# Layer 1's rotation: the halves of the partitions exchanged by ScalarE, one sine product on VectorE

## The reference, cut to what matters

```python
def _rope(x):
    ...
    freqs = jnp.repeat(freqs, 2, axis=-1)
    cos, sin = (jnp.cos(freqs), jnp.sin(freqs))
    x2 = x.reshape(*x.shape[:-1], DQ // 2, 2)
    rot = jnp.stack([-x2[..., 1], x2[..., 0]], axis=-1).reshape(x.shape)
    return x * cos + rot * sin
...
q = _rope(q)
k = _rope(k)
...
scores = scores + _alibi(t)[None]
scores = scores / math.sqrt(DQ)
scores = 30.0 * jnp.tanh(scores / 30.0)
...
probs = jax.nn.softmax(scores, axis=-1)
```

## Time and profile before

| what | value |
|---|---|
| median of 3 runs | 904.81 us (902.95 to 905.9) |
| profiled execution | 901.0 us, span 899.2 us |
| mean granted TensorE clock | 0.949 |
| PE / DVE / ACT / POOL busy | 804.3 / 626.3 / 448.5 / 466.3 us |
| chain that ended last | PE 67%, DVE 16%, POOL 7%, ACT 5% |

### The profile page before, as it was taken

One profiled execution on the slowest core, in us unless ns is written; L12 is line 12 of the kernel. 1 busy time (PEld: TensorE's weight loads), 2 busy tenths in 40 slices (PEclk: granted clock), 3 DMA queues, 4 the chain that ended last, 5 costly groups with the idle time before them and its releaser, 6 DMA issues.

```text
span 899.2 us, 13733 instructions
## 1 busy us (share of the span) xinstructions
PE 804.3 (89%) x4707; PEld 637.1 (71%) x4707; DVE 626.3 (70%) x1115; ACT 448.5 (50%) x795; POOL 466.3 (52%) x506
## 2 busy tenths in 40 slices
PE   2999999988787858998999897989999999999996
PEld 2866666663232246687888797979989998888874
DVE  8387757368988866789868884767766755555556
ACT  3322232188766622667645554555646552555541
POOL 3556736244654525445635547685866432565550
PEclk9999999997868987999999998999999999999999
DMA  4111192000000012000000001110110377754307
GB/s 173 54 52 35 53 315 75 1 1 0 1 1 1 2 37 107 25 7 7 25 7 19 7 18 49 31 48 25 48 36 25 115 166 286 216 150 117 95 3 233
DMA packets 50115, 59.80 MB, mean 67 GB/s; under 512 B 13559, under 2 KB 41084, under 8 KB 50048
## 3 DMA queue, kind: packets, MB, share of 16 engines
q1 hardware_dynamic: 45488, 50.49, 18.6%
q0 software_dynamic: 4560, 8.44, 2.6%
HBM read 41.11 MB, written 21.86 MB: 70 GB/s over the span
## 4 chain that ended last, share of the span: by engine, by line
PE 67%; DVE 16%; POOL 7%; ACT 5%; issue 4%; DMA 1%; SPq 0%; DVEq 0%; ACTq 0%; POOLq 0%
PE ps L452 11%; PE ps L454 10%; PE ps L453 10%; PE ps L693 9%; PE ps L778 7%; PE ps L596 6%; PE ps L802 3%; DVE A L1245 3%; DVE cap L1319 2%; DVE swap L1309 2%; PE ps L533 2%; PE ps L516 2%; PE ps L759 2%; PE ps L491 1%; POOL cT_lo L1633 1%
## 5 line engine op out<-in xcount | busy, mean ns | idle before, releaser
L993 ACT ACTIVATE cap<-cap 128x1024 f32<-128x1024 f32 (+7 forms) x128 | 86.8, 678 | 139.8 <-DVE cap L1319 139.5
L693 PE MATMUL ps<-V,P 128*128 128x129 f32 x1152 | 154.4, 281 | 0.0
L693 PEld LDWEIGHTS ps<-V,P 128*128 128x128 f32 x1152 | 147.1, 196 | 3.0
L1319 DVE SCALAR_TENSOR_TENSOR cap<-dist,ps 128x1024 f32<-128x1024 f32 (+7 forms) x128 | 95.9, 750 | 37.8 <-PE ps L454 25.8
L1529 POOL TENSOR_SCALAR_AFFINE_SELECT P<-P 128x128 f32<-128x128 f32 x128 | 38.5, 303 | 129.3 <-ACT P L998 129.1
L1659 POOL DMA_INDIRECT y_scratch<-y_sb,aux_s x63 | 62.0, 984 | 55.8 <-issue 38.9
L998 ACT ACTIVATE P<-cap 128x1024 f32<-128x1024 f32 (+7 forms) x128 | 87.6, 685 | 4.1
L452 PE MATMUL ps<-q_hi,k_hi 128*128 128x512 f32 x192 | 73.4, 382 | 4.1 <-DVE cap L1319 3.9
L1245 DVE TENSOR_TENSOR A<-A 128x1024 f32<-128x1024 f32 (+4 forms) x60 | 63.0, 1102 | 8.8 <-ACT A L942 8.5
L778 PE MATMUL ps<-ew,xT 128*128 128x256 f32 (+1 forms) x252 | 66.7, 387 | 2.6 <-ACT xT L1023 1.3
L454 PE MATMUL ps<-q_lo,k_hi 128*128 128x512 f32 x192 | 68.8, 358 | 0.0
(11 more groups left out here) (266 smaller groups left out, 2075.8 us busy)
## 6 DMA issues: line engine op xcount, KB each, us to landing
xg_scratch<-blank SPq DMA_DIRECT2D x1, 8127.0 KB, 31.7
xa<-xg_scratch SPq DMA_DIRECT2D x63, 128.0 KB
ew<-in_experts SPq DMA_DIRECT2D x3, 1920.0 KB, 7.7
ew<-in_experts SPq DMA_DIRECT2D x2, 2688.0 KB, 10.1
y<-y_scratch SPq DMA_DIRECT2D x8, 512.0 KB, 5.2
pk<-in_packed SPq DMA_DIRECT2D x8, 384.0 KB, 3.0
pks<-in_scales SPq DMA_DIRECT2D x8, 384.0 KB, 3.8
wqk<-in_wqk SPq DMA_DIRECT2D x20, 128.0 KB
```

The source lines that it names most:

```text
L693: last = pe.matmul(ps[:, 4 + r % 2, o:o + D1 + 1], P1[:, h % 2, a:a + P], V1[:, j, h // REP, :], start=(j == 0), stop=(j == t))
L993: act.activation(cap[:, n % 2, 0:w], cap[:, n % 2, 0:w], ACT.Tanh, scale=1.0 / (CAP * float(D1) ** 0.5))\
L1319: dve.scalar_tensor_tensor(out=cap[:, n % 2, 0:w], in0=dist[:, 0:w], scalar=slope, in1=psf[:, 1024 * (n % 2):1024 * (n % 2) + w], op0=ALU. ...
```

## The change

ScalarE gets a step for every projection, `swap_halves`: it waits for the projection and copies the upper half of the bank's partitions to the lower half of `swap` and the lower to the upper. VectorE waits for these copies (`pj_turned`) in place of the projection itself, multiplies the bank by the cosines as before, and then multiplies `swap` in place by the sines, in one instruction of 128 partitions with both inputs in SBUF. The sine table has the opposite sign on the two halves, so POOL subtracts where it added. `follow` puts the new step into ScalarE's list where the projection stands in `STEPS1`; the part steps stay in `later`. The wait that guards `swap` against POOL's reading moves from VectorE to ScalarE.

```diff
+            def swap_halves(n, half):
+                i = 2 * n + half
+                act.wait_ge(pj_ps, i + 1)
+                if i >= 2:
+                    act.wait_ge(pj_rot, i - 1)
+                b = ps[:, 6 + side_of["project", n, half] % 2, :]
+                for to, frm in ((slice(0, 64), slice(64, 128)), (slice(64, 128), slice(0, 64))):
+                    last = act.activation(swap[to, i % 2, :], b[frm, :], ACT.Copy)
+                last.then_inc(pj_turned, 1)
...
-                dve.wait_ge(pj_ps, i + 1)
+                dve.wait_ge(pj_turned, i + 1)
                 k = part_of["project", n, half]
                 if k >= 3:
                     dve.wait_ge(parts_ready, k - 2)
-                if i >= 2:
-                    dve.wait_ge(pj_rot, i - 1)
                 dve.tensor_tensor(rot[:, k % 3], b, cos1[:, tk], ALU.mult)
-                for to, frm in ((slice(0, 64), slice(64, 128)), (slice(64, 128), slice(0, 64))):
-                    last = dve.tensor_tensor(swap[to, i % 2, :], b[frm, :], sin1[frm, tk], ALU.mult)
-                last.then_inc(pj_cos, 1)
+                dve.tensor_tensor(swap[:, i % 2, :], swap[:, i % 2, :], sin1[:, tk], ALU.mult).then_inc(pj_cos, 1)
...
-                pool.tensor_tensor(r, r, swap[:, i % 2, :], ALU.add).then_inc(pj_rot, 1)
+                pool.tensor_tensor(r, r, swap[:, i % 2, :], ALU.subtract).then_inc(pj_rot, 1)
...
-            if engine == "dve" or (engine == "pool" and name == "project"):
+            if engine == "dve" or name == "project":
                 out.append(s)
```

More of the change, by code:

```diff
@@ L343, in build_program @@
         wqk_hi_ready, wqk_ready = sem("wqk_hi_ready"), sem("wqk_ready")
-        pj_ps, pj_cos, pj_rot = sem("pj_ps"), sem("pj_cos"), sem("pj_rot")
+        pj_ps, pj_turned, pj_cos, pj_rot = sem("pj_ps"), sem("pj_turned"), sem("pj_cos"), sem("pj_rot")
         parts_hi, parts_ready = sem("parts_hi"), sem("parts_ready")
@@ L1051, in _ @@
             for step in ACT_STEPS1:
-                {"project_part": project_part, "scores": scores, "turn_part": turn_part, "split_wqk": split_wqk,
-                 "split_wo": split_wo, "router": router, "moe": moe}[step[0]](*step[1:])
+                {"project": swap_halves, "project_part": project_part, "scores": scores, "turn_part": turn_part,
+                 "split_wqk": split_wqk, "split_wo": split_wo, "router": router, "moe": moe}[step[0]](*step[1:])
             for s in range(MOE_EARLY, NSTEP + 1):
```

## The result

The changed kernel takes 969.05 us in the median of 4 runs (967.1 to 972.98), the kernel before 903.88 in its 4 (902.65 to 905.9): a ratio of 1.0708 [1.0671, 1.0745], slower by 7%. The profiled execution took 969.04 us, with a span of 967.3 and a mean granted clock of 0.934.

The account below looks back on a forecast made before the run. Bound: each head step's loop of TensorE's scores, VectorE's bias add, ScalarE's tanh and exp, with ScalarE following. Terms 73.7, given back -5, clock +8: +77 on 901.0, 978; half of 3.8 added: 980 us, range 945 to 1006.

Parts of the forecast that it names:

- the forecast case: Whole kernel: the forecast itself, 980 us, with its own range of 962 to 990; chance 0.52.
- The mechanism: Layer 1's attention: copies follow tanh and exp, VectorE's rotation waits for them, the next bias add behind it; sum 73.7 us.
- the opening: Four projections opening layer 1's attention: each copy pair stands behind the previous projection's part copy; +3.1 us.
- what is given back: TensorE's slack (0.5 us) and ends of heads 7, 9, 11 already waiting for POOL: -5 us in all.
- the clock: TensorE idling within heads lowers its granted clock: five costs of 1.5 us, taken as 8; bounds 0 and 23.
- Head 13's two distances: Bias add's end to next one's start, first and second projection: 4.7 and 5.05 us, before 2.53 and 2.04.
- The copy: ScalarE's 64x512 copy from PSUM, 80 in all: taken at 0.60 us, two in a row 1.1.
- The two products: VectorE's cosine and sine product after the copies, in the chain between bias adds: 1.40 us at the first projection.
- Lighter VectorE wins: Rival, 13 loop projections of heads 0 to 3 and 5: 0.69 us saved each, -9, total 892; chance 0.03.
- the condition I had named: Loop projections: copies ready before VectorE arrives, if it has over 3.3 us of other work behind a bias add.
- Contention: Rival: 24 products with two SBUF inputs meet POOL's products, each losing 0.94 us, +22, total 1000; chance 0.08.
- TensorE's lead hides half: Rival: six heads with output projections absorb their delays (-17.4), no clock lost (-8), total 953; chance 0.18.

Follow-up runs that it names:

- the run with the wait alone: Kernel before, with VectorE's rotation in the loop also waiting for its own step's exponential, no added work: 941.18 us, ratio 1.0374.
- the run without the exchange: Kernel before, with one 128-partition sine product straight from PSUM replacing two of 64, halves not exchanged, no copies: 891.85 us, ratio 0.9867.
- the runs with the cosine product: Changed kernel, with VectorE's cosine product ahead of ScalarE's copies, only the sine product waiting for them: 954.1 us, ratio 1.0507.
- with the copies ahead: Changed kernel, with the copies ahead of the same step's tanh and exponential in ScalarE's list: 921.84 us, ratio 1.0172.

## Why the prediction was right

**Direction and size.** 980 was forecast, 945 to 1006 the range, 969.05 came: the forecast case, in its own range of 962 to 990. The mechanism was the one described, and the run with the wait alone shows it without the copies. That the total came so near is in part luck. On the profiled executions +77 was forecast and +68.1 came, but 6.9 of that lie ahead of the attention and behind the loop, where nothing was forecast. For the loop and the opening together the forecast was 76.7 and 61.2 came, so it was 15.5 too high; the range would still have held that (903.9 + 61.2 = 965). The excess lies in two terms, what is given back and the clock.

**The terms of the loop.** Head 13's two distances were forecast at 4.7 and 5.05 and are 4.65 and 4.95. The copy was taken at 0.60 and is 0.592, a pair at 1.1 and is 1.20. So half the partitions cost what all cost on ScalarE too (128x512 took 598 ns). The two products were taken at 1.40 and are 1.21, since the second starts 0.61 us after the first: this error and that of the copies nearly cancel. The opening was forecast at +3.1 and took 3.4. Over the heads, the terms add up to 70.6 (73.7 less the opening). The same distances between bias adds, read in both traces, grew by 69.3. The heads grew by 57.9, so some 11 us net came back in their other steps; for what is given back and the clock together the forecast was +3 (-5 and +8).

**What was given back** is the term that was too small. I had -5. TensorE's waits for POOL's low part at the ends of heads 7, 9 and 11, before and, below them, after (the changed kernel has none in 11):

```profile
554.42 0.58 PE L452 MATMUL ps<-wo_hi,cT_hi 128*128 128x256 f32 x1 [4.81 <-POOL cT_lo L1633]
605.03 0.58 PE L452 MATMUL ps<-wo_hi,cT_hi 128*128 128x256 f32 x1 [4.17 <-POOL cT_lo L1633]
653.83 0.39 PE L452 MATMUL ps<-wo_hi,cT_hi 128*128 128x256 f32 x1 [1.90 <-POOL cT_lo L1633]
```
```profile
594.85 0.39 PE L452 MATMUL ps<-wo_hi,cT_hi 128*128 128x256 f32 x1 [1.46 <-POOL cT_lo L1639]
651.63 0.39 PE L452 MATMUL ps<-wo_hi,cT_hi 128*128 128x256 f32 x1 [1.21 <-POOL cT_lo L1639]
```

The five waits of 12.8 us became two of 2.7, so 10.1 came back: the ends that POOL sets were delayed less than VectorE's chain. I had walked POOL's queue and allowed 1.0 to 1.6 a head; it was 3.35, 2.96 and 1.90. Heads 7, 9 and 11 lengthened by 2.3, 3.4 and 3.1 against 5.2, 7.6 and 5.2 before what is given back.

**The clock** was the other term, +8, and it doesn't show as an extra of that size. TensorE's time, busy us and granted clock in heads 5, 6 and 13, first before, then after:

```profile
479.08:503.26 24.18, 21.12 (x143) 1.00 0.02 6
503.26:532.72 29.46, 26.85 (x179) 0.94 0.07 19
...
681.18:700.22 19.04, 19.04 (x137) 1.00 0.00 1
```
```profile
510.38:539.12 28.74, 24.42 (x143) 0.88 0.02 6
539.12:568.96 29.84, 25.98 (x179) 1.00 0.06 18
...
736.20:762.34 26.14, 22.23 (x137) 0.87 0.00 0
```

In head 13 the clock fell from 1.00 to 0.87, and TensorE had an idle time there that before it hadn't:

```profile
749.10 0.80 PE L452 MATMUL ps<-q_hi,k_hi 128*128 128x512 f32 x1 [3.27 <-DVE cap L1325]
```

The same matmuls were busy 3.2 us longer, and the head lengthened by 7.1 where 5.2 was forecast. That is the episode I had priced, at 1.5. In head 6 the clock went the other way, 0.94 to 1.00, and the head lengthened by 0.4, not 2.3: before, an episode was already there. Over the loop TensorE was busy 12.7 us longer (332.8 to 345.5) for the same 2211 matmuls; how much of that reached the end the runs don't separate. The mistake was to add five episodes without subtracting those that the kernel before had: it shows 0.89 to 0.94 in heads 1, 2, 6, 7 and 9.

**The rivals.** *Lighter VectorE wins* failed in the changed kernel at the condition I had named, copies late for VectorE, and was right in what it would be worth: 892 was its price, 891.85 the run without the exchange. That the two agree so closely is luck: the price was -9 from heads 0 to 3 and 5, and these gave 6.4 of the loop's 14.1. *Contention* was to cost 0.94 in 24 products. The changed kernel's sine product, ns min, median and max:

```profile
L1316 DVE TENSOR_TENSOR swap<-swap,sin x40: 679/681/1507, 351.5 to 774.0; 128x512 f32<-128x512 f32 x40
```

Four of the 40 took 1000 to 1507 ns, each beside POOL's low part; the mean of 726 makes it 40 x 0.045 = 1.8 us in all. The rule of the Trainium skill (GPSIMD Engine Reference, Key points) agrees with these four and would have misled as a sum: the other 36 took some 0.68. The order decides how often it bites: the same product lost 6.0 and 5.6 us in the runs with the cosine product and with the copies ahead. *TensorE's lead hides half* was wrong where it was placed: the heads with output projections grew by 15.5, where the terms listed 18.3 for them (17.4 and the third projections of heads 6 and 10), while those that POOL ended absorbed more than I gave them.

## What to carry to other kernels

Before moving work to an engine with idle time, ask what stands ahead of it in that engine's list, and what stands behind the waiting instruction on the other engine: 42 us of copies were free when nobody waited for them and one added wait without any work cost 3.7%. Where the move is wanted, put it behind the other engine's result instead of in front of it, where only a late consumer needs it; that turned +7.1% into -0.7% with 72 of the 80 copies. And a place in a list has more than one client: moving the rotation behind the bias add freed ScalarE and starved TensorE of a bank. A product with two SBUF inputs also moves towards POOL's work or away from it: its 40 lost 1.8 us in one order and 6.0 in another.

## What was not expected of the hardware

ScalarE's copy of 64x512 took 592 ns from PSUM and 622 to 630 from SBUF (groups L985, L983 and L984): the source in SBUF is the slower one by 5 to 6%. A VectorE product with two SBUF inputs went from 693 to 2114 ns beside POOL, and the rotation's products that read PSUM never took over 694 in any of the runs. And single executions of the same program part differ by some 5 us ahead of layer 1 (the first projection matmul at 342.49 or 347.68), more than the 2.7 us that 0.3% of this kernel are.
